# An RWKV block with a ternary gate: the first activation load issued from SP instead of ACT

## What is computed

```python
prev = jnp.concatenate([x[:, 1:2, :], x[:, :-1, :]], axis=1)
xx = prev - x
xk, xv, xr, xg = x + xx * tm_k, x + xx * tm_v, x + xx * tm_r, x + xx * tm_g
r, k, v = xr @ Wr.T, xk @ Wk.T, xv @ Wv.T
g = jax.nn.sigmoid(xg @ Wg.T)
wkv = _wkv_scan(k, v, jnp.exp(-jnp.exp(time_decay)), time_first)
o = jax.nn.sigmoid(r) * wkv * g @ Wo.T      # then a layernorm over channels: s
# gate: silu(xn @ w_t.T * scale + bias), w_t the weight rounded to -1, 0, 1
# out = x + s * gate
```

## Time and profile before

| what | value |
|---|---|
| median of 2 runs | 1459.18 us (1457.33 to 1461.03) |
| profiled execution | 1461.05 us |
| its span, core 3, the slowest | 1459.5 us |
| spans of the eight cores | 1437.2 to 1459.5 us |
| PE busy | 824.0 us (56%) |
| DVE busy | 524.6 us (36%) |
| ACT busy | 494.2 us (34%) |
| DMA moved | 211.65 MB, mean 145 GB/s |

### The profile page before, as it was taken

One profiled execution on the slowest core, in us unless ns is written; L12 is line 12 of the kernel. 1 busy time (PEld: TensorE's weight loads), 2 busy tenths in 40 slices (PEclk: granted clock), 3 DMA queues, 4 the chain that ended last, 5 costly groups with the idle time before them and its releaser, 6 DMA issues. The chain is left out here.

```text
span 1459.5 us, 11807 instructions; the slowest of 8 cores (1437.2 to 1459.5 us)
## 1 busy us (share of the span) xinstructions
PE 824.0 (56%) x3834; PEld 361.6 (25%) x3834; DVE 524.6 (36%) x499; ACT 494.2 (34%) x660; POOL 105.1 (7%) x196
## 2 busy tenths in 40 slices
PE   3542210027939389999960794380597869884200
PEld 1110000014514145544420341130243424331000
DVE  0158998300010000767006054695410000000597
ACT  5532221212112121222212257466354333328221
POOL 0002222100000000011110000010000000000011
PEclk9999999999979689999985797795698989899555
DMA  4447888785152651556117433533624444300387
GB/s 124 137 135 260 248 259 218 188 246 161 61 174 78 218 177 47 182 168 192 43 37 258 126 114 100 143 102 115 198 91 125 121 125 122 114 15 0 105 250 221
DMA packets 79070, 211.65 MB, mean 145 GB/s; under 512 B 11424, under 2 KB 11424, under 8 KB 79008
## 3 DMA queue, kind: packets, MB, share of 16 engines
q1 hardware_dynamic: 54432, 139.57, 34.0%
q0 software_dynamic: 15360, 53.49, 10.3%
q10 hardware_dynamic: 9216, 17.83, 3.9%
HBM read 166.81 MB, written 39.85 MB: 142 GB/s over the span
## 5 line engine op out<-in xcount | busy, mean ns | idle before, releaser
L974 PE MATMUL rgo_ps<-mov_rg,rgo_wbf 128*128 128x512 bf16 x1024 | 235.1, 394 | 180.8 <-ACT rgo_wbf L821 59.8
L405 PE MATMUL g1ps<-mov_kv,g1wbf 128*128 128x512 bf16 (+1 forms) x1536 | 260.1, 334 | 110.8 <-DMA mov_kv<-sxk 46.3
L821 ACT ACTIVATE rgo_wbf<-rgo_mw 128x512 bf16<-128x512 f32 x192 | 120.0, 633 | 269.4 <-DMA rgo_mw<-wr 88.1
L405 PEld LDWEIGHTS g1ps<-mov_kv,g1wbf 128*128 128x128 bf16 x1536 | 132.7, 101 | 238.1 <-issue 122.1
L974 PEld LDWEIGHTS rgo_ps<-mov_rg,rgo_wbf 128*128 128x128 bf16 x1024 | 102.6, 101 | 313.3 <-issue 201.6
L974 PE MATMUL rgo_ps<-wkv_sb,rgo_wbf 128*128 128x512 bf16 x512 | 117.5, 394 | 25.4 <-ACT sr_sb L950 14.0
L405 PE MATMUL g1ps<-xn_sb,g1wbf 128*128 128x512 bf16 x512 | 110.7, 379 | 0.0
L269 DVE CAST g1wbf<-g1mwstg 128x1024 bf16<-128x1024 f32 x24 | 16.7, 694 | 247.4 <-PE g1ps L405 92.5
L333 ACT ACTIVATE g1row<-g1ps 128x512 f16<-128x512 f32 (+1 forms) x96 | 44.7, 492 | 146.0 <-PE g1ps L405 136.9
L573 PE MATMUL ps_sc<-fs_a,ones 128*1 128x512 f16 x64 | 32.3, 608 | 89.2 <-ACT fs_a L618 89.2
L974 PEld LDWEIGHTS rgo_ps<-wkv_sb,rgo_wbf 128*128 128x128 bf16 x512 | 51.3, 101 | 91.7 <-issue 35.8
(11 more groups left out here) (112 smaller groups left out, 842.2 us busy)
## 6 DMA issues: line engine op xcount, KB each, us to landing
g1mwstg<-wf SPq DMA_DIRECT2D x64, 512.0 KB, 4.7
g1mwstg<-wk SPq DMA_DIRECT2D x32, 512.0 KB, 7.9
g1mwstg<-wv SPq DMA_DIRECT2D x32, 512.0 KB, 4.9
rgo_mw<-wr SPq DMA_DIRECT2D x64, 256.0 KB, 3.4
rgo_mw<-wg SPq DMA_DIRECT2D x64, 256.0 KB, 3.2
rgo_mw<-wo SPq DMA_DIRECT2D x64, 256.0 KB, 3.4
xstg<-x SPq DMA_DIRECT2D x16, 576.5 KB, 4.0
xst<-x SPq DMA_DIRECT2D x16, 512.0 KB, 5.3
```

The costliest lines, as they stand in the source:

```text
L405: mm = e.matmul(bank[:, :t1 - t0], wbf[hh % 2][:, ic, oc * 128:(oc + 1) * 128], s["mov"][:, ic, t0:t1], start=(ic == 0), stop=(ic == CH - 1))
L821: e.activation(wbf[ss % 2][:, ic, :], mwstg[jj % 2][:, :], AF.Copy).then_inc(sem["scs"], 1)
L974: mm = e.matmul(bank[:, :t1 - t0], wbf[ss % 2][:, ic, oc * 128:(oc + 1) * 128], phs[p]["mov"][:, ic, t0:t1], start=(ic == 0), stop=(ic == ...
```

## The change

The call of `mm_group` gets `mov_sync={0: CH}`. With it, product 0 (wk) has all its 16 activation loads issued by SP at the very start of the stage, before any of the stage's weight loads, and ACT issues none of them. Product 1 (wv) is as before: its 16 loads are issued by ACT. The loads, their sizes, the semaphore and the counts waited for are the same.

```diff
-        ], sh, pre=dict(preL=CH, recs=g1_pre_recs))
+        ], sh, pre=dict(preL=CH, recs=g1_pre_recs, mov_sync={0: CH}))
```

## The result

| | us, median | runs |
|---|---|---|
| before | 1464.08 (1444.52 to 1515.34) | 39 |
| after | 1470.04 (1455.17 to 1527.01) | 40 |

The ratio is 1.0071, 95% interval 1.005 to 1.0092: the change makes the kernel slower by 7 to 13 us. That is within the 2% I had called no change, but it is clear of the noise of so many runs, and I had forecast +2. On 1459.18, the median before that the forecast started from, it makes 1469.5. Two later comparisons of the same kernel with fewer runs gave 1.003 (0.9986 to 1.0073) and 1.0038 (0.9983 to 1.0094); both intervals take in 1. (Ratios leave out runs in which one die was disturbed, and means over act_hold's cores leave out its cores 0 and 1 for the same reason; the table's medians and ranges leave out nothing.)

The account below looks back on a forecast made before the run. wk's slices, through ACT's casts ahead of its evictions, were taken to bound the stage. Core 3's +1.1 us and core 0's +4.9 became +2 on 1459.2, giving 1461.2 us; range 1454 to 1472.

Parts of the forecast that it names:

- forecast +2: Whole kernel: 2 us slower, taken between the results for cores 3 and 0, giving 1461.2 us.
- mov_kv 19 us after the barrier: Start of the wk stage, core 3: last mov_kv load landed 19 us after the barrier, instead of 31.4.
- the wait for ACT about 20 us: PE behind its eight full banks in wk: waits about 20 us for ACT's eviction, instead of 7.4.
- hardly a change by the clock: PE behind the longer pause: granted clock no worse than behind the short one, so nothing booked.
- Rival (a): PE starts wk 12.4 us earlier and the end moves with it: 1446.8 us; chance 0.04.
- +1.1 on core 3: Last ACT cast of wk's first half on core 3: 63.6 us after SP's start against 62.5, a loss of 1.1.
- +4.9 on core 0: Last ACT cast of wk's first half on core 0: 59.3 us against 54.4, a loss of 4.9.
- M: Time from the barrier to the last mov_kv landing; forecast 19 us on core 3, bounds 12.8 and 31.4.
- M + 44.6: Start of wk's last ACT cast: M plus 2 x 2.2 us for the first pair, 7 x 5.75 for seven more.
- the 62 to 66: Sign on core 3: last ACT cast 62 to 66 us after the barrier, then at 62.5.
- three to five: Sign on cores like core 0: last ACT cast three to five us later than before.
- Rival (c): Slower by the one queue: mov_kv lands late, M above some 22; 1466 us halfway, 1472.7 at the bound; chance 0.24.

Follow-up runs that it names:

- act_hold: Against the kernel before: ACT still issues mov_kv, but SP waits for all 16 loads to land before its first weight load; ratio 1.0031 (0.9984 to 1.0077).
- half_sp: Against the kernel before: first 8 of the 16 mov_kv loads on SP ahead of the weights, other 8 on ACT; ratio 1.002 (0.9975 to 1.0065).
- two_ahead: Against the kernel before: all 16 mov_kv loads on SP, behind the stage's first two weight loads; ratio 0.9997 (0.9959 to 1.0034).

## Why the prediction was wrong

What held. What bounds the stage's start is the arrival of wk's slices, through ACT's casts ahead of its evictions; mov_kv 19 us after the barrier (18.8 on core 3); the wait for ACT about 20 us (26.1); hardly a change by the clock: the granted clock of the 7.9 us behind the long pause was 0.73 against 0.77, both between the two levels, and from the last cast to the end of the half it took 44.0 us on core 3, where before it took 43.6 (means over the cores: 43.8 and 44.0). Rival (a) fell, as the rows had said. The window behind the pause, core 3, columns as in the earlier trace rows:

```profile
353.10:361.00 7.90, 7.84 (x39) 4.28 (x40) 0.00 (x0) 3.23 (x9) 1.08 (x2) 0.73 0.43 148
```

**The step that failed is the last one of the sum, "I take +2, between the two and nearer to core 3".** I had two results, +1.1 on core 3 and +4.9 on core 0, and leant on core 3 as the slowest. But core 3 was the core worst off at this very place: its mov_kv took 31.5 us, where the mean over the cores is 27.2 (24.0 to 31.5), and it had 62.6 us to the last cast, the other seven 54.5 to 60.1. Such a core has the least to lose by the change, and which core it is changes: in the second profile before it was core 4 (61.5), while core 3, again the slowest of the eight by its span, had 59.6. After the change the cores need M + 42.4 to M + 48.8. With the means the same sum gives 18.3 + 44.6 - 57.6 = +5.3.

**A second term was too small, M + 44.6.** On core 3 it was 67.6 - 18.8 = 48.8. The first ACT cast came 6.1 us behind mov_kv, not 4.4: in it are 1.28 us of ACT's table load, ahead of that cast, which I had left out. And a pair took (351.48 - 308.79) / 7 = 6.10 us, not 5.75. Over all cores it is 63.7 - 18.3 = 45.4, so this term is off by 0.8 at the mean: the first ACT cast is 5.5 behind mov_kv instead of 4.4, and a pair takes 5.7, as forecast. Two of the signs that the prediction named were missed with it: core 3's last cast at 67.6 lies above the 62 to 66, and core 0's moved by 7.0 (54.5 to 61.4) and not by three to five.

Together: +6.1 us in the first pair of profiles (63.7 - 57.6), and +6.4 over the two profiles before and the three after (64.2 - 57.9 at the last cast). The measured ratio is +7 to +13 us in the large comparison, and -2 to +14 in the two small ones. Some 6 of these us are shown. What is above is not settled. The wait for wf's second half, which came out longer in two of three profiles after, is a candidate for about one more. That the slowest of eight cores counts adds nothing: in the two small comparisons the mean of the eight spans grew by 5.0 and 9.7 us, the slowest core's by 4.0 and 8.0 (standard errors 1.2 and 1.6, and 2.5 and 3.2).

Rival (c), slower by the one queue, had the right sign and size (+7 at 0.24), but for a reason that did not come about: M stayed at 19. That 1469.5 lies inside the range of 1454 to 1472 is owed to (c), and so to luck, not to the sum. By the rule of the Trainium skill that the prediction cites (DMA: Bandwidth & Descriptors, section Issuing engines are not separate DMA queues) a second issuing engine saves only the issue time. act_hold agrees: with the order kept, the issuing engine made no difference (64.1 us to the last cast on ACT's queue, 63.7 to 65.2 on SP's). That the order of the loads matters, 6 us here, the rule leaves out.

## What to carry to other kernels

Before moving a load ahead of others, ask what the others feed: here a large load was running in the gaps of a two-buffer loop, and put in front of the loop it delayed the loop's first slice by 14 us (from 6.5 to 20.5) and its last by 6, to hasten something that was not waited for last. Where an in-order engine has work that waits (ACT's casts) ahead of work that frees others (its evictions), separate those first. That alone gave 2.8% here, more than any order of the loads, and the same move of the loads then turned from a loss of 6 us into a lead of 9.6 in the stage. And an effect that comes on every core is to be worked out at the mean of the cores, not on the one that happened to be slowest.

## What the runs showed of the hardware

Two full DMA queues were served side by side: with eight loads on each, a slice behind the eight on one came no earlier than behind 16 (20.7 and 20.5 us to the first cast), with four ahead at 14.1, with none at 6.5. By the Trainium skill (DMA: Bandwidth & Descriptors, section Queues, rings and completion order) each DMA engine goes round the queues that have work, a packet at a time. The runs agree that the queues take turns (eight loads each of half_sp, 9.5 and 10.4 us to landing at the median); that a turn is a packet none of them shows. The 16 issues took ACT 12.8 us at the mean of the cores before (9.4 to 15.5), beside SP's weights; they took SP 8.8 us after (8.2 to 9.7), and ACT 9.3 in act_hold, both with no weights beside them. In two_ahead, with two slices ahead in its own queue, SP took 8.5 to 14.3 us. The length went with what else was under way, not with the engine.
